# Routing results kept on chip, early gathers and weights, and a later last batch, at an attention-to-experts boundary

## The reference, cut to what matters

```python
x = x + L0_attn(layernorm(x))              # 16 heads of 16
x = x + L0_ffn(layernorm(x))               # experts, below
x = x + L1_attn(layernorm(x))              # phase attention
x = x + L1_ffn(layernorm(x))               # soft slots

def L0_ffn(x, gate_w, Wg, Wu, Wd):         # 8 experts, inner size 512
    affinity = softmax(einsum('bsd,de->bse', x, gate_w))
    gating, index = top_k(affinity.transpose(0, 2, 1), 256)   # 256 tokens per batch and expert
    x_sel = x[b_idx, index]
    h = silu(x_sel @ Wg[e]) * (x_sel @ Wu[e])
    contrib = (h @ Wd[e]) * gating[..., None]
    return zeros_like(x).at[b_idx, index].add(contrib)
```

## Time and profile before

| | us |
|---|---|
| median of 3 runs | 4881.25 |
| lowest, highest | 4877.01, 4888.4 |
| profiled execution | 4887.22 |
| its span, first to last instruction | 4885.4 |
| PE busy in the span | 4556.5 (93%) |
| DVE, ACT, POOL busy | 3270.8, 2206.4, 1148.4 |

### The profile page before, as it was taken

The page is one execution under the profiler, slowest core; times in us unless marked ns, Lnnn a source line. Parts: engine busy times, 40 slices in busy tenths (PEclk is TensorE's granted clock), DMA queues, the critical chain, the costliest instruction groups (busy, mean ns, idle before and its releaser), DMA issues. The chain is left out here.

```text
span 4885.4 us, 96760 instructions
## 1 busy us (share of the span) xinstructions
PE 4556.5 (93%) x40984; PEld 3133.7 (64%) x40984; DVE 3270.8 (67%) x3874; ACT 2206.4 (45%) x3585; POOL 1148.4 (24%) x854
## 2 busy tenths in 40 slices
PE   8699999999999996999996999949999999999999
PEld 5334444444333334888884455539999999988888
DVE  7599888887889861462223899956766666644443
ACT  3157777777677672323222555522222222233333
POOL 3512322222312202444441000003333333300000
PEclk9889999999999998999998999979999999999999
DMA  5544453544444316343344122256444444455553
GB/s 179 152 65 60 86 102 59 102 86 79 76 69 94 75 34 177 70 89 76 82 91 110 43 77 79 68 173 142 101 101 101 101 101 101 101 185 191 180 197 105
DMA packets 430317, 508.23 MB, mean 104 GB/s; under 512 B 29200, under 2 KB 361104, under 8 KB 421520
## 3 DMA queue, kind: packets, MB, share of 16 engines
q1 hardware_dynamic: 272272, 402.57, 31.3%
q10 hardware_dynamic: 133120, 67.12, 7.8%
q0 software_dynamic: 24576, 33.57, 4.2%
HBM read 250.25 MB, written 202.57 MB: 93 GB/s over the span
## 5 line engine op out<-in xcount | busy, mean ns | idle before, releaser
L974 DVE TENSOR_REDUCE att_nmx<-att_s 128x1 f32<-128x1024 f32 x1024 | 1206.4, 1216 | 183.1 <-PE att_s L797 178.8
L951 ACT ACTIVATE att_pt<-att_sT 128x512 f32<-128x512 f32 x2048 | 1083.2, 604 | 430.2 <-PE att_sT L853 426.8
L797 PE MATMUL att_s<-att_KT,att_QT 96*32 96x512 bf16 x8192 | 816.3, 393 | 92.5 <-DVE att_nmx L974 46.2
L853 PE MATMUL att_sT<-att_QT,att_KT 128*32 128x512 bf16 x8192 | 812.4, 384 | 6.2 <-ACT att_pt L951 4.9
L2658 POOL TENSOR_TENSOR sl_lg<-sl_lg,sl_sm 128x512 f32<-128x512 f32 x256 | 319.6, 1269 | 1318.8 <-DVE sl_sm L2808 1318.8
L868 PE MATMUL att_o<-att_pt,att_va 128*32 128x512 f32 x4096 | 540.5, 602 | 0.0
L797 PEld LDWEIGHTS att_s<-att_KT,att_QT 96*32 96x32 bf16 x8192 | 217.3, 97 | 494.8 <-DVE att_nmx L974 280.2
L2669 PE MATMUL sl_lp<-sl_phi,hand_big 128*128 (+1 forms) x4096 | 484.7, 277 | 30.9 <-DMA hand_big<-xnT 23.6
L2669 PEld LDWEIGHTS sl_lp<-sl_phi,hand_big 128*128 128x128 f32 x4096 | 472.2, 194 | 37.8 <-issue 35.9
L2915 PE MATMUL cb_op<-hand_big,cb_exT 128*128 128x256 f32 x2048 | 483.9, 380 | 0.0
L2733 ACT ACTIVATE sl_lg<-sl_lg 128x1024 f32<-128x1024 f32 x128 | 135.3, 1057 | 762.8 <-DVE sl_lg L2797 762.8
(11 more groups left out here) (312 smaller groups left out, 6201.0 us busy)
## 6 DMA issues: line engine op xcount, KB each, us to landing
lg<-sl_raw ACTq DMA_DIRECT2D x128, 512.0 KB, 6.0
hand_big<-lg SPq DMA_DIRECT2D x64, 1024.0 KB, 6.1
qk<-qkv_turned SPq DMA_DIRECT2D x64, 256.0 KB, 3.0
att_qin<-qk SPq DMA_DIRECT2D x64, 256.0 KB, 9.3
sl_w<-in_L_ffn_W SPq DMA_DIRECT2D x64, 256.0 KB, 3.6
y<-sl_y SPq DMA_DIRECT2D x16, 1024.0 KB, 6.9
hand_big<-y SPq DMA_DIRECT2D x7, 2048.0 KB, 8.5
att_QT<-att_hi SPq DMA_DIRECT2D x96, 128.0 KB, 4.4
```

Source lines behind the costliest of these rows:

```text
L797: ins = pe.matmul(bank[w * 32:(w + 1) * 32, q, :], QT[n % NB][0:ROWS, h, t * P + w * 32:t * P + (w + 1) * 32], KT[n % NB][0:ROWS, h, q * 5 ...
L853: ins = pe.matmul(sT[w * 32:(w + 1) * 32, at % 3, :], KT[g % NB][:, h, kt * P + w * 32:kt * P + (w + 1) * 32], QT[g % NB][:, h, step // 4 ...
L951: act.activation(pt[:, step % 2, h, c, :], sT[:, at % 3, :], ACT.Exp, scale=HD ** -0.5).then_inc(exp_done, 1)
L974: dve.tensor_reduce(nmx[n % 2][:, t, h:h + 1], s[i % 2][:].rearrange("p c k -> p (c k)"), AX.X, ALU.max, negate=True).then_inc(freed, 1)
```

## The change

A new outer stage, `Chosen`, lives over both `attend` and `experts`. It holds `ident`, `idx`, `wt`, the six `xg` buffers, and `wide`, whose four parts are buffers 2 and 0 of `QT` and `KT` in attention and later the weights of experts 0 and 1. It owns the semaphores `x_in`, `gu_in` and `wd_in`, all counting from zero. `idx` and `wt` are no longer stored and loaded. SP loads the weights of experts 0 and 1 in the last two attention turns, and POOL issues the first ten gathers (turns 0 to 4) at the end of its attention work. In `experts`, the steps of batch 7 come two turns later, and the bias row moves from turn 1 to turns 3 to 5, where PE waits for it behind `gate_up(5, 0)`. The weights of experts 2 and 3 take the places of 0 and 1 in SP's order, the latter behind `rb`.

```diff
+class Chosen:
+    NX = 6
+    def __init__(self, st):
+        self.ident = st.sb("ident", [P, P])
+        self.idx = st.sb("idx", [P, CAP // P, B * E], U32)
+        self.wt = st.sb("wt", [P, CAP // P, B * E])
+        self.xg = [st.sb(f"xg{j}", [P, CAP // P, D]) for j in range(self.NX)]
+        self.wide = st.sb("wide", [P, 4, HG * T // 2])
+        self.x_in = [st.pool_dma_sem(f"x_in{j}") for j in range(self.NX)]
+        self.gu_in = [st.pool_dma_sem(f"gu_in{e}") for e in range(E)]
+        self.wd_in = [st.pool_dma_sem(f"wd_in{e}") for e in range(E)]
...
+def expert_weights(eng, pick, e, tiles, wg_d, wu_d, wd_d):
+    for tile, src, sem in zip(tiles, (wg_d, wu_d, wd_d), (pick.gu_in[e], pick.gu_in[e], pick.wd_in[e])):
+        eng.dma_start(tile, src[e, :, :].rearrange("(k p) n -> p k n", p=P)).then_inc(sem, 16)
...
@@ attend @@
+        QT, KT = [[pick.operand(2 + j) if i == 0 else pick.operand(j) if i == 2 else st.sb(f"{name}{i}", [P, HG, T], BF16)
+                   for i in range(NB)] for j, name in enumerate(("QT", "KT"))]
...
+                    if n >= NG - 2:
+                        sp.wait_ge(st_done, FLOOR + SINGLES * n)
+                        expert_weights(sp, pick, n - (NG - 2), pick.expert(n - (NG - 2)), wg_d, wu_d, wd_d)
                     context_out(2 * n)
...
                 sp.dma_start(aff_d, aff[1][:]).then_inc(out_stored, 16)
-                sp.wait_ge(chosen, FLOOR + 2)
-                sp.dma_start(wt_d, wt[:]).then_inc(out_stored, 16)
-                sp.dma_start(idx_d, idx[:]).then_inc(out_stored, 16)
...
+                pool.wait_ge(chosen, FLOOR + 2)
+                pool.wait_ge(xn_stored, FLOOR + 16 * DONE)
+                for n in range(pick.NX - 1):
+                    for half in range(CAP // P):
+                        pool.indirect_dma_start(
+                            pick.xg[n][:, half, :], None, xn_d[0:DONE * T, :],
+                            bass.IndirectOffsetOnAxis(pick.idx[:, half, n:n + 1], 0)).then_inc(pick.x_in[n], 16)
...
@@ experts @@
-    PROJECT, NORMAL, TURN, GATE, ROWS, SEARCH, MERGE = 2, 4, 6, 8, 9, 10, 24
+    PROJECT, NORMAL, TURN, GATE, ROWS, SEARCH, MERGE = 4, 6, 8, 10, 11, 12, 26
+    BIAS_ROW = 4
...
-                sp.dma_start(idx[:, :, 0:R], idx_d).then_inc(c_in, 16)
-                sp.dma_start(wt[:, :, 0:R], wt_d).then_inc(c_in, 16)
-                sp.dma_start(ident[:], ident_d).then_inc(c_in, 16)
                 sp.dma_start(den[:], sums_of(den_d)).then_inc(den_in, 16)
-                weights(0)
+                weights(2)
                 sp.wait_ge(inverted, FLOOR + 1)
                 sp.dma_start(sums_of(rden_d), den[:]).then_inc(r_stored, 16)
-                weights(1)
...
+                weights(3)
                 sp.dma_start(nx[:], rows(x0_d, LAST)).then_inc(x0_in, 16)
...
-                for e in range(2, E):
+                for e in range(4, E):
                     weights(e)
...
-                pool.wait_ge(c_in, FLOOR + 48)
-                for n in range(NX - 1):
-                    gather(n)
...
                     gate_up(n, 0)
+                    if n == BIAS_ROW + 1:
+                        pe.wait_ge(row_ready, FLOOR + 1)
                     if n >= 1:
                         project_down(n - 1)
...
-                    if n == 1:
+                    if n == BIAS_ROW:
                         pe.wait_ge(spread, FLOOR + 1)
                         pe.wait_ge(row_in, FLOOR + 48)
+                        pe.wait_ge(y_ready, FLOOR + n - 1)
                         for k in range(KD):
-                            ins = pe.matmul(yp[1][:, 0, :], lnb_s[:, k, :], wo[:, k, :], start=k == 0, stop=k == KD - 1)
+                            ins = pe.matmul(yp[n % 2][:, 0, :], lnb_s[:, k, :], wo[:, k, :], start=k == 0, stop=k == KD - 1)
                         ins.then_inc(row_made, 1)
-                        pe.wait_ge(row_ready, FLOOR + 1)
...
                 dve.reciprocal(den[:], den[:]).then_inc(inverted, 1)
-                dve.wait_ge(row_in, FLOOR + 48)
-                for k in range(KD):
-                    ins = dve.tensor_copy(lnb_s[:, k, :], lnb[:, k:k + 1].broadcast_to([P, P]))
-                ins.then_inc(spread, 1)
                 for n in range(TURNS):
...
-                    if n == 1:
+                    if n == PROJECT - 1:
                         late_bias()
+                    if n == BIAS_ROW - 1:
+                        dve.wait_ge(row_in, FLOOR + 48)
+                        for k in range(KD):
+                            ins = dve.tensor_copy(lnb_s[:, k, :], lnb[:, k:k + 1].broadcast_to([P, P]))
+                        ins.then_inc(spread, 1)
```

More of the change, by code:

```diff
@@ L458, in attend @@
     with Stage(nc, "att") as st:
-        QT = [st.sb(f"QT{j}", [P, HG, T], BF16) for j in range(NB)]
-        KT = [st.sb(f"KT{j}", [P, HG, T], BF16) for j in range(NB)]
+        QT, KT = [[pick.operand(2 + j) if i == 0 else pick.operand(j) if i == 2 else st.sb(f"{name}{i}", [P, HG, T], BF16)
+                   for i in range(NB)] for j, name in enumerate(("QT", "KT"))]
         qin = [st.sb(f"qin{j}", [P, T]) for j in range(2)]
@@ L469, in attend @@
         va = [st.sb(f"va{j}", [P, NT, HG, 32]) for j in range(2)]
-        ident = st.sb("ident", [P, P])
+        ident = pick.ident
         identb = st.sb("identb", [P, P], BF16)
@@ L501, in attend @@
         step_s = st.sb("step", [P, 2, R])
-        wt = st.sb("wt", [P, 2, R])
-        idx = st.sb("idx", [P, 2, R], U32)
+        wt, idx = pick.wt[:, :, 0:R], pick.idx[:, :, 0:R]
         xn = rb[:].rearrange("p k t -> p (k t)").rearrange("p (t d) -> p t d", d=D)
@@ L1106, in choose @@
                     dve.wait_ge(merged, FLOOR + 5)
-                    dve.tensor_copy(idx[:], step_s[:]).then_inc(chosen, 1)
+                    dve.tensor_copy(idx, step_s[:]).then_inc(chosen, 1)
                 dve.wait_ge(c_in, FLOOR + 32)
@@ L1196, in experts @@
     with Stage(nc, "moe") as st:
-        ident = st.sb("ident", [P, P])
-        idx = st.sb("idx", [P, NS, B * E], U32)
-        wt = st.sb("wt", [P, NS, B * E])
-        wg = [st.sb(f"wg{e}", [P, KD, I]) for e in range(E)]
-        wu = [st.sb(f"wu{e}", [P, KD, I]) for e in range(E)]
-        wd = [st.sb(f"wd{e}", [P, NI, D]) for e in range(E)]
-        xg = [st.sb(f"xg{j}", [P, NS, D]) for j in range(NX)]
+        ident, idx, wt, xg, x_in, gu_in, wd_in = pick.ident, pick.idx, pick.wt, pick.xg, pick.x_in, pick.gu_in, pick.wd_in
+        here = lambda name, shape: [st.sb(f"{name}{e}", shape)[:] for e in range(2, E)]
+        wg, wu, wd = [[pick.expert(0)[m], pick.expert(1)[m]] + here(name, shape)
+                      for m, (name, shape) in enumerate((("wg", [P, KD, I]), ("wu", [P, KD, I]), ("wd", [P, NI, D])))]
         xT = [st.sb(f"xT{j}", [P, KD, CAP]) for j in range(2)]
@@ L1243, in experts @@
         yp = [st.ps(f"yp{j}", [P, NS, D]) for j in range(2)]
-        c_in = st.sem("c_in")
-        gu_in = [st.sem(f"gu_in{e}") for e in range(E)]
-        wd_in = [st.sem(f"wd_in{e}") for e in range(E)]
         row_in = st.sem("row_in")
@@ L1250, in experts @@
         row_ready = st.sem("row_ready")
-        x_in = [st.pool_dma_sem(f"x_in{j}") for j in range(NX)]
         turned = st.sem("turned")
@@ L1316, in weights @@
                 def weights(e):
-                    sp.dma_start(wg[e][:], wg_d[e, :, :].rearrange("(k p) n -> p k n", p=P)).then_inc(gu_in[e], 16)
-                    sp.dma_start(wu[e][:], wu_d[e, :, :].rearrange("(k p) n -> p k n", p=P)).then_inc(gu_in[e], 16)
-                    sp.dma_start(wd[e][:], wd_d[e, :, :].rearrange("(k p) n -> p k n", p=P)).then_inc(wd_in[e], 16)
+                    expert_weights(sp, pick, e, (wg[e], wu[e], wd[e]), wg_d, wu_d, wd_d)
                 def batch_in(b):
@@ L1504, in project_down @@
                     if n < E:
-                        pe.wait_ge(wd_in[e], FLOOR + 16)
+                        pe.wait_ge(wd_in[e], 16)
                     for s in range(NS):
@@ L1510, in project_down @@
                     ins.then_inc(down, 1)
-                pe.wait_ge(c_in, FLOOR + 48)
                 turn_tokens(0)
@@ L1598, in late_share @@
                     act.activation(ex[:], lgt[:], ACT.Exp).then_inc(exped, 1)
-                act.wait_ge(c_in, FLOOR + 48)
                 take_tokens(0)
@@ L3010, in build_program @@
     qkv_rope(nc, x0, a["wqk"], a["bqk"], a["L0_attn_Wv"], a["L0_attn_bv"], a["cos"], a["sin"], ident, qk, v)
-    attend(nc, qk, v, ident, a["kaug"], ctxT, den, rden, a["L0_attn_Wo"], a["L0_attn_bo"], x0, a["L0_ffn_gate_w"],
-           a["rowbase"], x1, xn, aff, idx, wt)
-    experts(nc, xn, idx, wt, a["L0_ffn_Wg"], a["L0_ffn_Wu"], a["L0_ffn_Wd"], ident, a["L1_attn_Wo"], a["L1_attn_ln_b"],
-            a["L1_attn_bo"], x1, xnT, x0, ctxT, den, rden, aff, a["rowbase"], a["L0_attn_Wo"], a["L0_attn_bo"],
-            a["L0_ffn_gate_w"])
+    routed = [a["L0_ffn_" + n] for n in ("Wg", "Wu", "Wd")]
+    with Stage(nc, "pick") as st:
```

(5 more changed lines are left out.)

28 lines of the change are left out of this document (16 added, 12 removed).

## The result

The changed kernel takes 4849.69 us (median of 4 runs, 4846.68 to 4855.2), the kernel before on the same chip 4884.82 us (4 runs, 4877.01 to 4891.22): ratio 0.9932, 95% interval 0.9919 to 0.9945. The forecast was 4848. The profiled execution took 4855.2 us with a span of 4853.4, against 4887.22 and 4885.4 before.

What follows compares the result with a forecast made beforehand. Experts taken as PE bound once running, time winnable only near the attention boundary. Gains 0.8 + 1.4 + 11.4 + 18.7 + 4.9 = 37.2, less 3.8 and 0.3, give 33.1 off 4881.25: 4848 us, range 4836 to 4861.

Steps and rivals of the forecast that it cites:

- part 1: End of attention: only the store of aff is left, so the last landing comes sooner; gain 0.8 us.
- part 2: Entry into the experts: POOL raises 17 fewer of 75 semaphores while all engines wait; gain 1.4 us.
- part 3: Indices and first gathers: PE starts with the barrier, the gathers ending before attention's exit; gain 11.4 us.
- Part 4: Loading weights of experts 0 and 1 in the last two attention turns: cost 0, bound 0 to 2 us.
- Part 5: Early experts: spreading lnb in turn 3 removes the hT stall, 16.0 us, and its slow restart, 2.7 us.
- Part 6: Wait for moe_bo ahead of turn 2, moved behind gate_up(5,0): gain 3.1 us plus 1.8 of slow matmuls.
- Part 7: Last batch two turns later: turn 10 collides with batch 0's statistics, PE's stall grows to 3.1 us; loss 3.8, bound 0 to 5.
- Part 8: One more semaphore clear on POOL before the next stage: loss 0.3 us, bound 0.1 to 0.8.
- Supply: Loads for turns 2 to 4: awo through near 1882, bias row near 1895, expert 4 near 1901, one to ten us margin.
- the stall moves: Rival, chance 0.14: loads still late, PE waits 1 to 5 us at turn 4; gain 25 to 29, 4852 to 4856.
- the start does not move: Rival, chance 0.11: something else at the experts' entry takes the 11.4 us; gain 21.7, 4859.5 us.
- Slower: Rival, chance 0.02: transfers bound the early expert turns and the gain is lost; 4891 us.

Runs made afterwards that it cites:

- shift_one: Changed kernel with the last batch's steps one turn later than before instead of two: 4860.9 us, ratio 0.9947 to the kernel before.
- weights_late: Changed kernel with the weights of experts 0 and 1 loaded in the experts stage, in SP's old order: 4878.65 us, ratio 0.9986 to the kernel before.
- row_early: Changed kernel with the bias row made in turn 1 again and lnb spread ahead of turn 0: 4872.8 us, ratio 0.998 to the kernel before.
- share_first: Changed kernel with ACT issuing the exponential for the late aff ahead of batch 0's deviation in turn 10: 4845.98 us, ratio 0.9927 to the kernel before.
- after: The changed kernel itself, without further edits, in its first profile: median 4849.69 us, ratio 0.9932 to the kernel before.
- after_again: The changed kernel, unedited, run once more on a third chip: 4865.09 us, ratio 0.9959 to the kernel before.
- batch_early: Changed kernel with batch 7's steps back at their old turns, the bias row staying late: 4852.15 us, ratio 0.9941 to the kernel before.
- raise_ahead: Changed kernel with the experts' semaphores raised by POOL behind its attention work, not between the stages: 4855.98 us, ratio 0.9934 to the kernel before.

## Why the prediction was right, point by point

- **Parts 1 to 3, 13.6 us: measured 13.5.** From the end of the last product the semaphore clear comes 6.45 us later before and 5.7 after (part 1, 0.8); 58 raises take 4.8 us for 6.1 (part 2: 1.3 for 1.4); the first transpose comes at the barrier (11.29 idle, "11 to 12" said). The bound in part 3, that the gathers end ahead of the exit, holds in every profile. What the sum left out is the other direction, a gather that slows the attention beside it: no row of before shows POOL gathering beside attention, and I gave it no bound. On two of the four chips it cost 10.7 us, a third of the gain. "I am wrong if the attention stage gets longer" is met there, and the test for it in part 3, a gather of more than 1.95 us, could not see it: the gathers stand 1.25 us apart in shift_one too.
- **Part 4, 0 with bound 2: right as an added cost, wrong as a statement of its worth.** weights_late shows 14.3 us of waits, 0.8 of them there anyway, that the early loads take away. The sum for parts 3 and 5 holds only with them, and the text should have priced the cover.
- **Part 5, 16.0 + 2.7.** No wait for `hT` of that kind is left, DVE stands at none of `row_in`, `num` and `late_in`, and row_early brings the wait back with 22.3. In the second profile of before it is 12.7, so the term is 13 to 16 by the execution.
- **Part 6, 4.9.** No wait for `moe_bo` at PE, no slow products at turn 2. No run takes this part back by itself.
- **Part 7, loss 3.8: measured 4.5, less 1.7 found beside it.** The wait is 3.00, said 3.1. The 16 products behind it span 6.2 us for 3.6, so 2.6 and not 1.8. Against that the gate's products ahead of it are cheaper than in before by 1.7 (3.64, 2.52 and 3.07 for 4.50, 3.76 and 2.63). The wait and its chain are as predicted, and share_first bears them out. The step that tied the clock's drop to a wait of this size doesn't hold as a rule: it was followed by slow products in three of seven profiles with that wait, so the 1.8 came near by luck. The two table loads in the chain take 1.28 us each with the next ACTIVATE at once. By the 2.66 us of the Trainium skill (ScalarE: Activation LUTs, "What ACT_TABLE_LOAD costs") the wait would, as an estimate, have been some 2.8 us longer, 5.9; it was 3.00, so this trace disagrees with the page.
- **Part 8, 0.3: not shown.** From the end of the experts' last product to the next stage's first it is 27.11 us in before and 27.45 in after, but 27.59 in the second profile of before.
- **Supply.** `awo` was through at 1879.3, said 1882, which is 1 us later than said once the earlier start of 4 us is taken off. The last load of the bias row was issued at 1884.35 and landed at 1890.1; expert 4's gate weights were issued at 1885.51 and landed at 1891.7, some five us sooner than said with that shift taken off. PE never waits for a weight. The rival "the stall moves" fell with this, and "the start does not move" with the first transpose. "Slower" by the transfers was nearest to what weights_late shows, 14 us of waits and still not slower than before.
- **Sum.** 13.5 + 21.4 less 0.3 is 34.6 on the path of the profiled pair, for 33.1 predicted. By terms the 21.4 are 18.7 + 4.9 - 4.5 + 1.7 = 20.8, and 0.6 stay unassigned. The medians differ by 35.1. That all three lie within 2 us is partly luck: the other pairs of profiles give down to 24.9 for 34.9, and of the two cases in which the gathers stretch attention or not, the measured one was the one without. Two slips in the working change nothing: four turns of 11 us from 1859.2 end at 1903.2, and the chances of the four cases that are faster add up to 0.95.
- **What the range missed.** The same kernel has a median of 4865 in after_again, above the range's upper end of 4861: the range had no place for a cost that one chip shows and another doesn't.

## What to carry to other kernels

When work is moved ahead of a barrier, price three things: the way that it leaves (here 13.5 us), the next wait on the path (row_early: 24 of 35 us were lost while it stood), and the loads that its old lateness had hidden (weights_late: 14 us). Move only as much as the first turn needs: two gathers did what ten did but for a wait of 0.9 us, and were free of the 10.7 us. Look also at what the barrier itself does, since raising semaphores where POOL is idle was worth 4.9 us for a few lines. And profile each kernel twice before reading a difference of a few us: here two profiles of one kernel differed by 3.3 and by 6.6 us over the same stretch.

## What was not expected of the hardware

- Ten indirect gathers on POOL (0.95 us each, 1.25 us apart) beside attention left ACT and PE untouched in four profiles (16.0 us for the stretch) and held them up in five (26.6 to 27.1), with ACT waiting up to 5.20 us. The four timed runs of after_again without a profile fit it (4862 to 4866). Two gathers didn't do it.
- SP's issue of one load of the same size and place, `awo`, took 12.27 us in before, 9.86 in after and 6.30 in batch_early; in weights_late it took 0.99 and the next load's issue 9.08. My reading, which no run tests: the issue that meets the backlog of the queue is the one that blocks.
- After the same wait of 3.00 us at the same place the products of TensorE ran at the lower of its two clocks in after (3.62 for eight) and at the upper in raise_ahead (1.89); over all profiles with this wait it was three to four.
